# Attention: the products with the values go two blocks at a time, behind every eighth transposed score

## The reference, cut to what matters

```python
q = _rope(proj(Wq, bq))
k = _rope(proj(Wk, bk))
v = proj(Wv, bv)
scores = jnp.einsum('bhqd,bhkd->bhqk', q, k) / jnp.sqrt(jnp.asarray(HEAD_DIM, dtype=x.dtype))
attn = jax.nn.softmax(scores, axis=-1)
ctx = jnp.einsum('bhqk,bhkd->bhqd', attn, v)
```

## Time and profile before

| | us |
|---|---|
| median of three runs | 6240.07 |
| lowest, highest | 6239.82, 6246.85 |
| the profiled execution | 6243.18 |
| its span in the trace | 6241.3 |

### The profile page before, as it was taken

One profiled execution on the slowest core, in us unless ns is written; L12 is line 12 of the kernel. 1 busy time (PEld: TensorE's weight loads), 2 busy tenths in 40 slices (PEclk: granted clock), 3 DMA queues, 4 the chain that ended last, 5 costly groups with the idle time before them and its releaser, 6 DMA issues. The chain is left out here.

```text
span 6241.3 us, 91686 instructions
## 1 busy us (share of the span) xinstructions
PE 5427.8 (87%) x30989; PEld 3414.3 (55%) x30989; DVE 3589.0 (58%) x5224; ACT 2170.5 (35%) x3509; POOL 1632.1 (26%) x1327
## 2 busy tenths in 40 slices
PE   6799999999999854999947667569999998999999
PEld 4433333333333453888833334269999995555555
DVE  7788888888888545111147787768888881000000
ACT  1057777777777420222214333221111111111111
POOL 3822222222222201444403454313333330000000
PEclk9889999999999956999958788779999999999999
DMA  5400000000000371333360101171011012111111
GB/s 201 156 15 14 20 21 20 21 18 16 21 20 21 129 274 40 71 68 61 55 221 27 51 30 54 61 271 43 29 36 36 29 43 76 34 57 34 44 34 37
DMA packets 352415, 390.78 MB, mean 63 GB/s; under 512 B 55795, under 2 KB 313843, under 8 KB 351731
## 3 DMA queue, kind: packets, MB, share of 16 engines
q1 hardware_dynamic: 275830, 263.08, 13.7%
q10 hardware_dynamic: 51840, 92.29, 3.9%
q0 software_dynamic: 24576, 33.57, 3.3%
HBM read 237.70 MB, written 151.18 MB: 62 GB/s over the span
## 5 line engine op out<-in xcount | busy, mean ns | idle before, releaser
L662 DVE TENSOR_REDUCE att_mx<-att_s 128x1 f32<-128x512 f32 x2112 | 1306.1, 681 | 145.1 <-PE att_s L542 141.2
L643 ACT ACTIVATE att_pt<-att_sT 128x512 f32<-128x512 f32 x2048 | 1078.9, 599 | 431.6 <-PE att_sT L571 431.4
L542 PE MATMUL att_s<-att_KT,att_QT 96*128 96x512 bf16 x2112 | 821.3, 392 | 29.0 <-DVE att_mx L662 15.3
L571 PE MATMUL att_sT<-att_QT,att_KT 128*128 128x512 bf16 x2048 | 749.3, 384 | 18.1 <-ACT att_pt L643 17.2
L1993 DVE RECIPROCAL cb_rs<-cb_op 128x4 f32<-128x4 f32 x16 | 2.9, 182 | 1004.8 <-PE cb_op L1965 1004.8
L583 PE MATMUL att_o<-att_pt,att_va 128*32 128x512 f32 x4096 | 544.5, 604 | 6.5 <-DVE att_osb L717 6.5
L542 PEld LDWEIGHTS att_s<-att_KT,att_QT 96*128 96x128 bf16 x2112 | 206.6, 98 | 620.2 <-DVE att_mx L662 469.0
L1711 POOL TENSOR_TENSOR sl_lg<-sl_lg,sl_sm 128x512 f32<-128x512 f32 x256 | 319.6, 1269 | 836.9 <-DVE sl_sm L1843 836.9
L1722 PE MATMUL sl_lp<-sl_phi,sl_xT 128*128 (+1 forms) x4160 | 490.4, 277 | 27.2 <-DMA sl_xT<-xnT 22.6
L1965 PE MATMUL cb_op<-cb_y,cb_ex 128*128 x2048 | 512.2, 393 | 0.0
L1940 PE MATMUL cb_lp<-cb_xT,cb_phi 128*128 128x512 f32 x1036 | 488.7, 594 | 25.5 <-DMA cb_xT<-xnT 25.5
(11 more groups left out here) (229 smaller groups left out, 7834.8 us busy)
## 6 DMA issues: line engine op xcount, KB each, us to landing
xnT<-n_xnT ACTq DMA_DIRECT2D x64, 512.0 KB, 5.8
n_x<-x SPq DMA_DIRECT2D x27, 1024.0 KB, 10.8
att_gin<-qkv SPq DMA_DIRECT2D x34, 768.0 KB, 4.9
qkv<-qkv_y ACTq DMA_DIRECT2D x64, 384.0 KB, 2.4
xn<-n_xn ACTq DMA_DIRECT2D x24, 1024.0 KB, 9.6
cb_y<-y SPq DMA_DIRECT2D x9, 2048.0 KB, 10.4
sl_w<-in_L_ffn_W SPq DMA_DIRECT2D x68, 256.0 KB, 3.7
y<-sl_y SPq DMA_DIRECT2D x16, 1024.0 KB, 7.0
```

Source lines behind the costliest of these rows:

```text
L542: pe.matmul(s1[:, u % 3, :], QT[par][0:ROWS, h, t * P:(t + 1) * P], KT[par][0:ROWS, h, c * 512:(c + 1) * 512], start=True, stop=True).then ...
L571: pe.matmul(sT[:, idx % 3, :], KT[par][:, h, kt * P:(kt + 1) * P], QT[par][:, h, s // 4 * 512:(s // 4 + 1) * 512], start=True, stop=True). ...
L643: act.activation(pt[:, (s % 2) * HG + h, c], sT[:, k % 3, :], ACT.Exp, scale=HD ** -0.5).then_inc(exp_done, 1)
L662: dve.tensor_reduce(mx2[:, t, h, c:c + 1], s1[:, u % 3, :], AX.X, ALU.max).then_inc(maxed, 1)
```

## The change

The two blocks of step s - 1 are both issued behind the eighth transposed score of step s; behind the fourth none is issued any more. The blocks of step 7, at the group's end, stay where they were.

```diff
@@ -609,8 +609,9 @@
                             if place in at_place:
                                 score_unit(n, par, at_place[place])
                             if h == HG - 1:
-                                if s > 0:
-                                    times_v(g, j, s - 1, c)
+                                if s > 0 and c == 1:
+                                    times_v(g, j, s - 1, 0)
+                                    times_v(g, j, s - 1, 1)
                                 if place + 1 in at_place:
                                     score_unit(n, par, at_place[place + 1])
                         times_v(g, j, STEPS - 1, 0)
```

## The result

The changed kernel takes 6333.19 us in the median of four runs (6327.58 to 6334.49), the kernel before 6243.46 us in the same comparison. The ratio is 1.0141, with a 95% interval from 1.0124 to 1.0159: 1.4% slower, where 6323 us and a range of 6290 to 6360 were predicted.

What follows compares the result with a forecast made beforehand. TensorE sets the attention stage's pace, with VectorE close behind. Losses of 2.66 us in 24 groups and 2.36 us in 8 make 83 us, so 6323 us, 1.3% slower; range 6290 to 6360.

Steps and rivals of the forecast that it cites:

- step 7: Last step of a group, only four scores: exponentials bound it, so the transposes of the maxima come 0.20 us later.
- The price of the banks: Three score banks: after two blocks without a score between, VectorE's next maximum starts 0.94 us late, once a step.
- steps 4 and 6: Second half of a group, VectorE bounds: plus 0.47 us (nine scores) and plus 0.77 us (with the division).
- step 5: Second half of a group, with VectorE's copy of the sums: 7.66 us against 6.87, plus 0.79.
- The steps: Each runs from the score behind its last product block to the next such score; losses sum to 2.66 us a group.
- Step 1: Start of a group, VectorE's run of maxima already full: the score after the double block comes 0.35 us later.
- steps 2 and 3: First half of a group, two part transposes each: 7.06 us against 7.02, plus 0.04 each.
- The gain on TensorE: Joining two product blocks saves 0.09 + 0.12 = 0.21 us, seven times a group, 1.47 us.
- The wait for the copy: The first block of step 5 waits 0.28 us for VectorE's copy of the sums; moved half a step later, this goes.
- The term of 2.36 us for groups after a drop of the clock: Loss per group where VectorE starts Step 1 emptier, taken as one group in four, 8 in all.
- Rival (c), the clock: Slower than forecast: TensorE's new waits bring one clock drop in every group of the attention stage, 6359 us; chance 0.10.
- Rival (a), faster: Joined blocks' saving comes through and the banks cover the gap: 56 us gained, 6184 us; chance 0.07.

## Why the prediction was right, point by point

- **The price of the banks** (0.94 us late once a step) holds. In the trace's way of counting, from the end of the last maximum, it is 0.87 us in steps 4 and 6 and 1.02 in step 5; the prediction counted from when the next maximum could have begun, which is 0.08 us before that end. Short maxima took the loss away, a fourth bank took 0.60 us off it in the one place where nothing else bound, and a score between the blocks left it in place. VectorE's wait for scores was forecast at about 190 us and is 204.2.
- **The steps**: forecast plus 0.35, 0.04, 0.04, 0.47, 0.79, 0.77, 0.20; measured 0.33, 0.04, 0.04, 0.46, 0.82, 0.75, 0.19 from the rows above and the earlier trace rows. Step 1 is taken from its first score in both. The sum for steps 2 and 3 has a slip: 17 x 0.22 + 0.90 is 4.64, not 4.67, and with the waits 4.89, which is what the trace has (996.51 to 1001.40). It leaves the 7.06 as it is, since the double block took 0.02 us less.
- **The gain on TensorE**, 0.21 us per pair, is real: the double block takes 1.86 us to the next score where I had 1.88, and with short maxima step 4 falls from 5.90 to 5.67. In the changed kernel it is eaten by the waits for banks, in step 7 by the exponentials.
- **The wait for the copy**, 0.20 to 0.28 us at the first block of step 5, is gone: the trace shows no idle time ahead of that block. It was worth nothing here, since VectorE bounds that step. In the kernel before, with the division moved already, taking it away gave 0.27 us.
- **The total** came out 10 us above the 6323 forecast. Of these 3.4 us are the kernel before, whose median was 6243.46 in this comparison and not 6240.07. The difference of the two kernels is 90 us against 83: 84 in the attention stage, and the rest in stages that the change does not touch. The term of 2.36 us for groups after a drop of the clock fits what is seen (57.3 to 59.5 us), and the groups at a turn's start without a drop gained 2.6 us like the others.
- **Rival (c), the clock**: not borne out. The Trainium skill, "TensorE: Matmul & The Clock Gate", A second HAM failure mode, tells of a kernel whose clock went up and down with brief idle times of TensorE between groups of matmuls. The new waits for PSUM banks did not bring that here: the stage has 0.99 before and after. Drops at every turn appear in one kernel only, the one with short maxima and joined blocks, and they stand at the starts of turns, not at the waits for banks.
- **Rival (a), faster**: right about TensorE, wrong about the cover. The rule of the Trainium skill, "TensorEngine Tiling (Array Packing)", Key Properties, that a change of the tiling mode drains TensorE, agrees with the 0.09 and 0.12 us at the two edges of a block, though no run separates a drain from another cause of them. It is small beside what VectorE loses.

## What to carry to other kernels

Where one queue feeds two consumers through rings of buffers, price a reordering by the longest stretch in which one of them gets nothing, against the work its ring can hold, less the time that it takes to hand a bank over. Here three banks are 1.80 us of maxima. A score starts 0.13 us after the 0.60 us of the maximum that frees its bank, and its own maximum starts 0.42 us behind it, so 1.25 us from one score to the next are covered. One block makes that 1.31 us, the balance of before; two make it 2.19, and 0.94 are lost. Fewer switches between kinds of matmul saved 0.2 us each, and cost up to 0.8 where the consumer was close to the limit. The same closeness read the other way gives the gain: a copy and a division taken out of VectorE's chain made the kernel 0.4% faster.

## What I had not expected of the hardware

The drops of the granted clock to its lower level came in very different number in kernels that differ little. With the maxima halved and the blocks apart it dropped near the start of 7 turns, with the blocks joined at all 15 behind the first; before and after the change, 8 and 9 times; with four banks for the scores, 3 times. These are counts of one profiled execution each. Before and after the change TensorE had stood idle for 1.6 to 1.9 us in the turn's first microseconds each time, as in the earlier trace rows, but it does that at turns without a drop too, so what decides is open. A group with a drop is about 1.5 us longer in the kernel before, 1.2 after the change, and 0.8 with the division moved. Differences below some 12 us between totals of this kernel are therefore better read in the groups without a loop start, which repeat within 0.05 us.
